# Cross-attention block and RWKV-style block on one core: the four mixes of a batch issued as two pairs, v with w and k with r

## What is computed

```
xa  = layernorm(x)                                  # b, 256, 256
sx  = previous token of xa - xa                     # the first one from a state
xxx = tanh((xa + sx * maa_x) @ maa_w1)              # 5 groups of 32 features
xxx = einsum('blfd,fde->blfe', xxx, maa_w2)         # the five "mixes": 32 -> 256 each
xk, xw, xv, xr, xg = xa + sx * (maa_stack + xxx)
w = exp(-exp(time_decay + tanh(xw @ td_w1) @ td_w2))
r, k, v = xr @ Wr.T, xk @ Wk.T, xv @ Wv.T
g = silu(xg @ Wg.T)
# per head of 8: s = k (x) v + w * s, out = r . (u * k (x) v + s), over the tokens
x1 = x + groupnorm(out) * g @ Wo.T
return x1 + sigmoid(xr2 @ Wfr.T) * (relu(xk2 @ Wfk.T)**2 @ Wfv.T)
```

## Time and profile before

| | us |
|---|---|
| median of 3 runs | 532.79 |
| lowest, highest | 532.39, 741.87 |
| the profiled execution | 532.36 |
| its span in the trace | 530.6 |
| PE busy in it | 442.5 |
| DVE busy | 328.6 |
| ACT busy | 213.2 |
| POOL busy | 111.8 |

### The profile page before, as it was taken

How to read it: one execution, slowest core, us unless ns; L and a number is a source line. 1 busy time by engine, 2 the same in 40 slices (tenths; PEclk the granted TensorE clock), 3 DMA queues, 4 the chain that set the end, 5 groups by cost and what they waited for, 6 DMA issues and landing times.

```text
span 530.6 us, 7006 instructions
## 1 busy us (share of the span) xinstructions
PE 442.5 (83%) x2628; PEld 266.0 (50%) x2628; DVE 328.6 (62%) x592; ACT 213.2 (40%) x409; POOL 111.8 (21%) x103
## 2 busy tenths in 40 slices
PE   4988888888989989889989989899999796860655
PEld 2652243434765444467644544675564584540444
DVE  1257666563347577846768788447797444399653
ACT  1440065566425436541443547336368431130202
POOL 7330231300000041301004102402054300063400
PEclk9996599999999989999996999999999997575869
DMA  7889965554002722200062103000611000330001
GB/s 255 278 265 366 316 180 180 157 151 111 1 0 74 168 60 62 61 1 1 20 160 61 41 20 101 2 0 1 148 32 41 2 0 0 94 85 0 0 1 40
DMA packets 24696, 46.91 MB, mean 88 GB/s; under 512 B 2484, under 2 KB 18772, under 8 KB 23256
## 3 DMA queue, kind: packets, MB, share of 16 engines
q1 hardware_dynamic: 23672, 44.94, 29.5%
q10 hardware_dynamic: 992, 1.54, 0.9%
HBM read 31.63 MB, written 14.68 MB: 87 GB/s over the span
## 4 chain that ended last, share of the span: by engine, by line
PE 64%; DVE 23%; ACT 7%; issue 4%; DMA 1%; POOL 1%; SPq 0%; DVEq 0%; ACTq 0%; POOLq 0%
PE pW L414 10%; DVE mx L932 9%; PE pO L473 8%; PE pMX L441 7%; PE pST L456 7%; PE pW L558 5%; PE pW L549 5%; PE pW L586 4%; PE pW L487 4%; ACT probs L678 4%; DVE A L897 4%; PE pW L500 3%; PE pW L422 2%; PE pW L635 1%; DVE A L1052 1%
## 5 line engine op out<-in xcount | busy, mean ns | idle before, releaser
L932 DVE TENSOR_REDUCE mx<-pMX 128x1 f32<-128x512 f32 (+1 forms) x192 | 122.9, 685 | 43.7 <-PE pMX L441 42.5
L678 ACT ACTIVATE probs<-pST 128x512 f32<-128x512 f32 x192 | 103.9, 597 | 50.0 <-PE pST L456 48.7
L441 PE MATMUL pMX<-Kst,Qst 97*128 97x512 bf16 (+1 forms) x256 | 73.4, 358 | 22.9 <-DVE mx L932 21.6
L473 PE MATMUL pO<-probs,Vn 128*32 128x256 f32 x768 | 62.6, 398 | 0.9 <-ACT probs L678 0.4
L456 PE MATMUL pST<-Qst,Kst 99*128 99x256 bf16 x384 | 59.8, 279 | 0.8 <-ACT probs L678 0.8
L441 PEld LDWEIGHTS pMX<-Kst,Qst 97*128 97x128 bf16 x256 | 21.1, 100 | 68.9 <-DVE mx L932 53.9
L897 DVE TENSOR_TENSOR_SCAN A<-four,COL,A 128x256 f32<-128x256 f32 x64 | 49.7, 838 | 0.0
L456 PEld LDWEIGHTS pST<-Qst,Kst 99*128 99x128 bf16 x384 | 32.4, 99 | 34.2 <-ACT probs L678 16.5
L487 PE MATMUL pW<-hT,Wkq 128*128 128x256 f32 (+1 forms) x96 | 33.6, 502 | 7.4 <-DMA Wkq<-w_kq 7.1
L549 PE MATMUL pW<-T,Wup 128*128 128x256 f32 x128 | 29.0, 381 | 1.8 <-DVE SX L1101 1.2
L1087 DVE SCALAR_TENSOR_TENSOR A<-pW,COL,SX 128x256 f32<-128x256 f32 x32 | 14.0, 479 | 25.3 <-PE pW L586 25.3
(11 more groups left out here) (135 smaller groups left out, 599.0 us busy)
## 6 DMA issues: line engine op xcount, KB each, us to landing
Kst<-k_stack SPq DMA_DIRECT2D x16, 576.0 KB
A<-v_rows SPq DMA_DIRECT2D x8, 1024.0 KB, 9.0
k_stack<-A SPq DMA_DIRECT2D x8, 576.0 KB, 3.1
k_stack<-A SPq DMA_DIRECT2D x8, 384.0 KB, 2.9
Qst<-q_stack SPq DMA_DIRECT2D x16, 192.0 KB
hT<-hT SPq DMA_DIRECT2D x3, 768.0 KB, 4.8
q_stack<-A SPq DMA_DIRECT2D x16, 128.0 KB, 3.1
Wsq<-w_sq SPq DMA_DIRECT2D x1, 2048.0 KB, 14.0
```

Of the source, the lines that this page charges most:

```text
L441: last = mm(pMX[n % 2][:, at:at + hi - lo], Qst[s][0:R_MASK + 1, h, qt * P:(qt + 1) * P], Kst[s][0:R_MASK + 1, h, lo:hi], start=True, stop ...
L473: last = mm(pO[32 * j:32 * j + 32, 0:TQ], Vn[b % 2][:, at:at + 32], probs[(n + j // 2) % UNITS_P][:, j % 2, :], start=nt == 0, stop=nt == ...
L678: act_fn(probs[n % UNITS_P][:], pST[n % ST_BANKS][:], ACT.Exp, scale=1.0 / DH)\
L932: v.tensor_reduce(dst, src, AX.X, ALU.max).then_inc(max_done, 1)
```

## The change

A new kind of step, "pair", stands in `TAIL` for two mixes: mix_vw and mix_kr. It counts as two units and so claims both banks: first one and then the other, before any matmul. Then PE issues for each half c the matmul of the first kind and that of the second, into the two banks; each kind signals after its last matmul. DVE reads both banks in one step, first kind first. The adds stay post steps, maag moves behind td1, mix_g stays a unit. The order string was rewritten with it. In the listing the whole order string is cut to its first changed lines.

```diff
--- before.py
+++ after.py
@@ -65,8 +65,8 @@
 TAIL = (("x", "-"), ("oT", "A"), ("proj", "D"), ("sq", "-"), ("rms", "-"), ("z", "-"), ("zT", "A"),
         ("up0", "A"), ("up1", "A"), ("up2", "A"), ("up3", "A"), ("down", "D"),
         ("stat1", "-"), ("root1", "-"), ("z2", "-"), ("xaT", "A"), ("sx", "-"), ("xin", "-"), ("maa1", "A"),
-        ("mix_v", "D"), ("add_v", "-"), ("mix_w", "D"), ("v", "A"), ("add_w", "-"), ("mix_k", "D"), ("add_k", "-"),
-        ("maag", "A"), ("td1", "A"), ("k", "A"), ("mix_r", "D"), ("add_r", "-"), ("td2", "A"), ("decay", "-"),
+        ("mix_vw", "2"), ("add_v", "-"), ("add_w", "-"), ("v", "A"), ("mix_kr", "2"),
+        ("add_k", "-"), ("add_r", "-"), ("td1", "A"), ("maag", "A"), ("k", "A"), ("td2", "A"), ("decay", "-"),
         ("mix_g", "D"), ("add_g", "-"), ("r", "A"), ("kv1", "-"), ("kv0", "-"), ("ruk", "-"), ("scan00", "-"),
         ("rs00", "-"), ("g", "D"), ("scan01", "-"), ("rs01", "-"), ("scan10", "-"), ("rs10", "-"), ("diag", "D"),
         ("scan11", "-"), ("rs11", "-"), ("gate", "-"), ("wkv", "A"), ("ojT", "D"), ("gsq", "-"), ("gated", "-"), ("gvar", "-"), ("groot", "-"), ("gout", "-"),
@@ -75,8 +75,8 @@
 TAIL_NAMES = {n for n, _ in TAIL}
 KQ = ("kq00", "kq01", "kq10", "kq11")
 VP = ("vp0", "vp1", "vp2")
-READS_LAST = {n: who for n, who in TAIL if who != "-"}
-READS_LAST.update({n: "D" for n in KQ + ("oq", "vb")}, **{n: "A" for n in VP + ("m",)})
+READS_LAST = {n: who for n, who in TAIL if who in "AD"}
+READS_LAST.update({n: "D" for n in KQ + ("oq", "vb", "mix_v", "mix_w", "mix_k", "mix_r")}, **{n: "A" for n in VP + ("m",)})
 
 
 
@@ -120,17 +120,16 @@
 
 
 def tail_stream(b):
-    return [("unit" if who != "-" else "post", n, b) for n, who in TAIL]
+    return [({"-": "post", "2": "pair"}.get(who, "unit"), n, b) for n, who in TAIL]
 
 
 ORDER = ("k6 v5 s k5 m v m s2 m5 k v m29 0 1 k2 s k3 x2 m2 x2 m4 x2 s2 m3 k x5 m4 x3 m3 x m3 x m x2 m3 k4 s m2 k m x3 "
          "k x m3 x2 m3 x2 m2 x3 m x m2 x m x m x2 m2 x4 m2 x3 m2 x11 m 02 m3 03 v 0 m3 02 m2 03 m 03 v2 m3 0 s2 0 x2 "
-         "m4 x m x3 s 02 m2 03 x3 m2 04 x m2 04 m x2 02 m3 x3 m3 02 x2 m2 x2 m x m7 s2 x2 07 m x3 m x 0 x7 m6 x4 0 m x "
...
+         "m4 x m x3 s 03 m2 0 x3 m2 04 x m3 x2 05 m3 x3 m3 02 x2 m2 x2 m x m7 s2 x2 07 m x3 m x 0 x7 m6 x4 0 m x 02 m "
...
 
 
 def schedule():
@@ -145,7 +144,14 @@
 
 
 STEPS = list(schedule())
-UNIT = {s[1:]: i for i, s in enumerate([s for s in STEPS if s[0] == "unit"])}
+
+
+def units_of(step):
+    kind, name, b = step
+    return [(name, b)] if kind == "unit" else [("mix_" + k, b) for k in name[4:]]
+
+
+UNIT = {u: i for i, u in enumerate([u for s in STEPS if s[0] in ("unit", "pair") for u in units_of(s)])}
 ORDER = sorted(UNIT, key=UNIT.get)
 
 
@@ -288,7 +294,7 @@
             return ROW[:, ROWS[name], :][:, None, :].to_broadcast([P, n, E])
 
         def tail_of(step):
-            return TAILS[TAIL_SET[step[2]] if step[0] in ("unit", "post") and step[1] in TAIL_NAMES else 0]
+            return TAILS[TAIL_SET[step[2]] if step[0] in ("unit", "pair", "post") and step[1] in TAIL_NAMES else 0]
 
         def tiles(ap):
             return ap.rearrange("p (a n) -> p a n", a=2)
@@ -473,6 +479,17 @@
                         last = mm(pO[32 * j:32 * j + 32, 0:TQ], Vn[b % 2][:, at:at + 32],
                                   probs[(n + j // 2) % UNITS_P][:, j % 2, :], start=nt == 0, stop=nt == STAGES - 1)
                     last.then_inc(pv_done, 1)
+                elif kind == "pair":
+
+                    _, name, b = step
+                    taken(pe, "maa1", b)
+                    banks = [(MIX[k], claim("mix_" + k, b)) for k in name[4:]]
+                    for c in range(C):
+                        for f, bk in banks:
+                            last = mm(bk[:, c * TQ:(c + 1) * TQ], Wmaa2[f * DM:(f + 1) * DM, c * P:(c + 1) * P],
+                                      X.xob[f * DM:(f + 1) * DM, 0, :], start=True, stop=True)
+                            if c == C - 1:
+                                last.then_inc(unit_ready, 1)
                 elif kind == "unit":
                     _, name, b = step
                     if name[:2] == "kq":
@@ -574,16 +591,12 @@
                         for c in range(C):
                             last = mm(bk[0:DM, 0:TQ], Wmaa1[:, c, P:NF * DM], X.T[:, c, :], start=c == 0, stop=c == C - 1)
                         last.then_inc(unit_ready, 1)
-                    elif name[:4] == "mix_":
-                        f = MIX[name[4]]
-                        taken(pe, "maag" if f == 4 else "maa1", b)
-                        bk = claim(name, b)
-                        for c in range(C):
-                            if f < 4:
-                                lhs, rhs = Wmaa2[f * DM:(f + 1) * DM, c * P:(c + 1) * P], X.xob[f * DM:(f + 1) * DM, 0, :]
-                            else:
-                                lhs, rhs = Wmaa2g[:, c * P:(c + 1) * P], X.xob[0:DM, 1, :]
-                            last = mm(bk[:, c * TQ:(c + 1) * TQ], lhs, rhs, start=True, stop=True)
+                    elif name == "mix_g":
+                        taken(pe, "maag", b)
+                        bk = claim(name, b)
+                        for c in range(C):
+                            last = mm(bk[:, c * TQ:(c + 1) * TQ], Wmaa2g[:, c * P:(c + 1) * P], X.xob[0:DM, 1, :],
+                                      start=True, stop=True)
                         last.then_inc(unit_ready, 1)
                     elif name in ("v", "k", "r", "g"):
                         if b == 0 and name == "v":
@@ -917,6 +930,14 @@
                         last.then_inc(newton, 1)
                 return last
 
+            def mixed_in(k, b, view):
+
+                f = MIX[k]
+                for c in range(C):
+                    last = v.scalar_tensor_tensor(X.mixed[k][:, c, :], view[:, c, :], col("stack", f * C + c),
+                                                  X.SX[:, c, :], ALU.add, ALU.mult)
+                last.then_inc(taken_by["D"], 1)
+
             for step in STEPS:
                 kind = step[0]
                 X = tail_of(step)
@@ -1021,6 +1042,15 @@
                     elif name == "out":
                         taken(dve, "fv", b)
                         v.scalar_tensor_tensor(X.Z, X.G2, 0.5, X.xob, ALU.mult, ALU.add).then_inc(did["fo"], 1)
+                elif kind == "pair":
+                    _, name, b = step
+                    if name == "mix_vw":
+                        if b == 0:
+                            dve.wait_ge(kq_out, SPILLS * 16 * B)
+                        else:
+                            ready(dve, "wkv", b - 1)
+                    for k in name[4:]:
+                        mixed_in(k, b, tiles(ready(dve, "mix_" + k, b)[:]))
                 elif kind == "unit":
                     _, name, b = step
                     if name == "m":
@@ -1076,17 +1106,8 @@
                     elif name == "down":
                         dve.wait_ge(did["xb"], b + 1)
                         v.tensor_tensor(X.xb2, view, X.xb2, ALU.add).then_inc(taken_by["D"], 1)
-                    elif name[:4] == "mix_":
-                        f = MIX[name[4]]
-                        if name == "mix_v":
-                            if b == 0:
-                                dve.wait_ge(kq_out, SPILLS * 16 * B)
-                            else:
-                                ready(dve, "wkv", b - 1)
-                        for c in range(C):
-                            last = v.scalar_tensor_tensor(X.mixed[name[4]][:, c, :], view[:, c, :],
-                                                          col("stack", f * C + c), X.SX[:, c, :], ALU.add, ALU.mult)
-                        last.then_inc(taken_by["D"], 1)
+                    elif name == "mix_g":
+                        mixed_in("g", b, view)
                     elif name == "g":
                         dve.wait_ge(did["th"], b + 1)
                         v.scalar_tensor_tensor(X.G2, X.TH, 1.0, view, ALU.add, ALU.mult)\
```

## The result

The changed kernel takes 548.96 us (median of 4 runs, 544.29 to 553.02) against 533.02 before, a ratio of 1.0301 with a 95% interval of 1.0252 to 1.0351: slower by 16 us. The ratio leaves out 553.02 and, of the kernel before, 741.87, which lie far above the fastest execution of their kernel. The profiled execution took 550.17, its span is 548.4.

A forecast was written before the change was run, and what follows sets the result against it. PE, busy 83%, was taken as the likeliest bound. Batches 0 to 3 (+5.1, +3.8, +0.6, +2.0) and clock (+1.0) sum to 12.5 over 532.36, giving 544.9, stated as 544.5 us; range 536 to 551.

The forecast's parts named there:

- (a): Before v/w pair: PE idles for maa1's tanh, 0.64 us in batch 0, 1.7 in batch 1, 0.75 in batch 2.
- (d): DVE reads r at once, so M reductions queue behind both reads and add_k: 2.35 us idle before M101, batch 0.
- (c): Before k/r pair: it claims v's bank, so both mixes wait for ACT's copy of v; 0.85 us idle per batch.
- rival 2: Clock falls at every new gap: 5 us in all in place of 1.0, batch 3 at 2.8; about 549; chance 0.17.
- Rival 4: Pairs don't run at once: each costs the old 2.12 us, savings of 6.2 lost; about 551; chance 0.04.
- (b): Unit behind v/w waits for DVE's reads: m.3 2.5 us (batch 0), vp1 1.1 (batch 1), xcT 1.05 (batch 2).
- The row M137 to M143: Batch 1: these fills, no longer divided by maag, td1 and k, last 2.0 us longer than PE's own work.
- rival 3: Lag partly given back: DVE catches up during PE's idle, half of the 8.9 us returns; about 539; chance 0.20.
- the two reasons named: Batch 3: DVE reads w besides v, then does stat2 of batch 2, before add_v; v starts 1.9 us later.
- my upper case of 2.8: Batch 3: mix_g's read comes 2.8 us later if the clock stays low for td1 and maag, otherwise 1.1.
- one drop, 1.0: Clock: one fall to 1.2 GHz somewhere beside the new idle, adding 1.0 us, with 0 and 4 as ends.
- Rival 1: Whole kernel: packing wins, the waits are filled and only savings of 6.2 us stay; about 526; chance 0.08.

## Why the prediction was right, and where its sizes were off

**The direction and the mechanism** held: in an order in which PE has nothing to do behind maa1 and v, it waits at (a) to (d), and these waits are longer than what the pairs save. Single mixes in the same order (1.0238) show that it is the order that costs and not the joint claim; of the terms only (c) spoke of that claim. The median lies in the range, but 0.96 above the 541 to 548 that had most of the chance: the 544.5 was 4.5 too low, and what came is rival 2.

**Savings.** A pair holds PE for 1.07, I took 1.10. Rival 4 (no concurrency) is out, by the trace: a pair in 1.07 and not 2.12.

**(a) tanh.** Predicted 0.64, 1.7, 0.75 of idle; the waits read 0.56, 1.57, 0.56. **(b)** 2.5 before m.3: 2.28. vp1 1.1: 0.97. xcT 1.05: 1.06. vp2 1.1: 0.93. **(c)** 0.85: 0.78 in every batch. **(d)** 2.35 before M101: 1.94.

Two terms of batch 1 were wrong and cancelled, which was luck. The row M137 to M143 was to last 2.0 longer; it takes 3.80 (280.44 to 284.24) where the same fills in two rows took 3.50 before, 0.3 more. And of the 1.8 of idle PE that was to fall away, the 1.4 of waits for maxima is still there. v's wait for the copy of vp1, 0.4 in the sum, does not show at the slow clock and is 0.3 with the waits filled. In rival 3 half of 8.9 taken from 544.5 is 540, not 539.

**The sum without the clock.** I had 5.1, 3.8 and 0.6 for batches 0 to 2; the kernel with filled waits shows 4.4, 3.4 and 0.3. Batch 3: 2.0 predicted, 3.0 measured. v started 1.7 later behind the tanh where I had 1.9, for the two reasons named; td1 and maag ran at the low clock, which was my upper case of 2.8. Rival 3 wanted half of the lags of batches 0 and 1 given back. At the window ends the lag is 7.2, 12.9, 14.0 and 17.0, and 17.8 at the end of the span. By more than 0.1 it shrinks only between batches 1 and 2, by 1.8, where the kernel before has its slow stretch from 280.8 to 291.1; that this stretch is the cause is my reading and not shown by a run.

**The clock** is the term that was mis-sized. I took one drop, 1.0. There were drops behind the gaps in all three batches (the P steps at 1.08, the windows at 0.80, 0.89 and 0.84), and they cost 9.2 in the windows, while between the windows 1.9 came back. Net 7.3 in place of 1.0. This is rival 2: it had 5 of clock and 2.8 for batch 3 and gave 549, against 548.96. That it agrees so closely is luck: its clock was 2 too low and its waits 1.3 too high, and the four executions lie 9 us apart. For the profiled execution: waits less savings 8.2, batch 3 3.0, clock 7.3, less 0.7 at the two ends, which is the 17.8 by which the span grew. This is bookkeeping and not a test, because the part of the clock between the windows is what remained there. What tests the clock is the run with filled waits: the same order with more work on PE has 1.00 in all three windows and a ratio of 1.0166 (1.0098 to 1.0234) against 1.0301 (1.0252 to 1.0351).

Not every drop has idle PE ahead of it, though. In the kernel before the clock fell at 280.8, and PE had waited for nothing since 274:

```profile
276.95 1.12 PE L586 MATMUL pW<-xob,Wmaa 32*128 32x256 f32 x4
...
279.13 1.10 PE L586 MATMUL pW<-xob,Wmaa2g 32*128 32x256 f32 x4
...
280.70 1.00 PE L473 MATMUL pO<-probs,Vn 128*32 128x256 f32 x8
```

From 276.95 to 280.16 it ran matmuls of 32 and 64 rows alone, and the P step behind them already takes 1.00. This stretch and the one at 192.1 were left out of the sum, which reads the clock only in the windows of the mixes.

**Rival 1** (the packing wins once the waits are filled) had 0.08. With filler in front of the pairs the whole is still slower: 1.0134, and 1.0021 against 0.9896 with the tail's clock up. In single stretches at full clock the gain is there, 0.45 us in batch 0.

What stays open: how the loss of the pairs behind filler splits between the low clock of batch 1, DVE's block of four reads and the claims. Pairs behind filler together with unread matmuls in batches 0 to 2 would tell the clock's part, and might be no slower than the kernel before; neither that nor a version in which DVE reads w and r later, as separate steps, was tried.

## What to carry to other kernels

Before two units are set side by side, count the banks: with two banks in turns, the second unit or the one behind it stands until a reader is through, whether the two are claimed together (1.0301) or one by one (1.0238). Steps that look like clutter between two dependent units are what hides the latency; list them before moving one. And price idle PE twice, once for the wait and once for the matmuls behind it at half clock: where a wait can't be removed, useless matmuls into a free bank were worth 1 to 1.4% here. Read the clock outside the changed stretches too, in the kernel before as well.

## What was not expected of the hardware

- Matmuls on different row groups ran at once whether they alternated or came one kind after the other: 1.07 us for eight records both ways, 1.06 for four.
- A gap of 1.6 us in batch 1 and one of 2.3 us in batch 0, beside 32-row matmuls, were followed by 1.2 GHz; in batch 2 the gaps ahead of the drop were 0.92 before maa1 and 0.56 before the pair. At that level a P step takes 1.08 in place of 0.64, and v's projection 3.78 in place of 1.89.
- The clock also fell with no wait of PE ahead of it, behind 3.2 us of matmuls of 32 and 64 rows (the kernel before, 280.8).
- Slow stretches are not tied to a place in the program. Those of the kernel before at 192 and 280 are not in the trace of the changed kernel, which has others at 214 and 323, and the kernel before itself took 526.66 to 533.32 in 19 executions on one chip, with a mean granted clock of 0.938 in the fastest and 0.916 to 0.923 in those over 532.
